# First output blocks of the last batch, worked inside the last attention unit and between the last attention products

## The reference

```python
scale, shift = split(emb @ W_emb + b_emb)             # emb is cond
xn = rms_norm(x, g_norm) * (1 + scale) + shift
q, k, v = heads(xn @ W_qkv);  q, k = rms_norm(q, g_q), rms_norm(k, g_k)
o = softmax(q @ k.T / 8) @ v                           # per head
x = x + o + o @ W_out
x = x + (causal depthwise conv1d(x, w=cond, 4 taps) + b_conv)
```

## Time and profile before

| | before |
|---|---|
| time, median of 3 executions | 2622.6 us (2620.4 to 2622.89) |
| the profiled execution | 2618.81 us |
| its span | 2616.9 us |
| mean granted TensorE clock | 0.958 of full |
| PE busy | 2372.9 us, 91% |
| DVE busy | 2106.6 us, 80% |
| ACT busy | 1815.4 us, 69% |
| POOL busy | 660.5 us, 25% |

### The profile page before, as it was taken

How to read it: one execution, slowest core, us unless ns; L and a number is a source line. 1 busy time by engine, 2 the same in 40 slices (tenths; PEclk the granted TensorE clock), 3 DMA queues, 4 the chain that set the end, 5 groups by cost and what they waited for, 6 DMA issues and landing times.

```text
span 2616.9 us, 54024 instructions
## 1 busy us (share of the span) xinstructions
PE 2372.9 (91%) x20690; PEld 1527.4 (58%) x20690; DVE 2106.6 (80%) x3360; ACT 1815.4 (69%) x2823; POOL 660.5 (25%) x460
## 2 busy tenths in 40 slices
PE   1458998888889999999999999999999999999698
PEld 0034555555556666666666666666666666666487
DVE  6757777777778888888888888888888888888845
ACT  2237777777777877777777778777777777877611
POOL 0052322223222233222233232332222222222000
PEclk8879989989989999999999999999999999999789
DMA  6877988989999999999999999999988989887841
GB/s 236 344 192 152 172 166 174 180 173 179 218 197 183 185 203 184 193 190 219 205 206 193 200 187 189 196 186 229 193 176 171 179 162 182 165 164 155 158 150 61
DMA packets 1234881, 487.07 MB, mean 186 GB/s; under 512 B 1139521, under 2 KB 1196993, under 8 KB 1232065
## 3 DMA queue, kind: packets, MB, share of 16 engines
q1 hardware_dynamic: 1234624, 483.63, 87.8%
HBM read 141.13 MB, written 57.18 MB: 76 GB/s over the span
## 4 chain that ended last, share of the span: by engine, by line
PE 69%; DVE 11%; issue 6%; ACT 4%; SPq 3%; DMA 1%; POOL 0%; ACTq 0%; DVEq 0%
PE proj L774 36%; PE scores L723 11%; PE values L742 10%; PE proj L798 8%; DVE neg L1178 5%; DVE p_pair L1187 4%; SPq L576 3%; ACT p_pair L896 2%; PE proj L801 1%; PE misc L811 1%; DVE bias L1181 1%; ACT prob L888 1%; PE misc L786 1%; PE values L757 1%; PE values L749 1%
## 5 line engine op out<-in xcount | busy, mean ns | idle before, releaser
L774 PE MATMUL proj<-w_sb,xn_sb 128*128 128x384 f16 x6144 | 1029.4, 327 | 33.9 <-DMA xn_sb<-p_pair 29.1
L888 ACT ACTIVATE prob<-scores,bias,l_scale 128x1024 f32<-128x1024 f32 x512 | 615.5, 1203 | 353.7 <-DVE bias L1181 336.0
L774 PEld LDWEIGHTS proj<-w_sb,xn_sb 128*128 128x128 f16 x6144 | 588.9, 98 | 434.0 <-DMA xn_sb<-p_pair 25.6
L1178 DVE TENSOR_REDUCE neg<-scores 128x1 f32<-128x1024 f32 x512 | 623.8, 1218 | 156.1 <-PE scores L723 152.3
L1187 DVE TENSOR_TENSOR p_pair<-prob,p_pair 128x1024 f16<-128x1024 f32 x512 | 614.8, 1242 | 137.6 <-ACT p_pair L896 137.6
L896 ACT ACTIVATE p_pair<-prob 128x1024 f16<-128x1024 f32 x512 | 511.0, 1049 | 0.4 <-DMA pT<-p_pair 0.4
L723 PE MATMUL scores<-stack 64*128 64x512 f16 x3072 | 391.4, 389 | 58.8 <-ACT prob L888 57.1
L742 PE MATMUL values<-pT,v_pair 128*64 128x256 f16 x6144 | 396.9, 280 | 11.0 <-DMA pT<-p_pair 6.3
L742 PEld LDWEIGHTS values<-pT,v_pair 128*64 128x64 f16 x6144 | 324.2, 112 | 93.5 <-issue 78.6
L1102 POOL TENSOR_TENSOR rs<-ms,power 128x16 f32<-128x16 f32 x64 | 185.6, 2900 | 395.6 <-DVE ms L1201 395.6
L1131 POOL TENSOR_TENSOR oT_pair<-oT,oT_pair 128x256 f16<-128x256 f32 x128 | 148.7, 1162 | 541.4 <-ACT oT_pair L965 541.4
(11 more groups left out here) (127 smaller groups left out, 2089.3 us busy)
## 6 DMA issues: line engine op xcount, KB each, us to landing
w_sb<-w_dram SPq DMA_DIRECT2D x128, 384.0 KB, 4.1
o_dram<-oT_pair SPq DMA_DIRECT2D x128, 128.0 KB, 2.5
out<-acc SPq DMA_DIRECT2D x64, 256.0 KB, 2.7
wq_raw<-in_L_cond_W_qkv SPq DMA_DIRECT2D x8, 1536.0 KB, 10.6
w_dram<-wq_pair SPq DMA_DIRECT2D x8, 1536.0 KB, 7.4
x_in<-in_x SPq DMA_DIRECT2D x24, 512.0 KB, 4.4
oT_in<-o_dram SPq DMA_DIRECT2D x12, 1024.0 KB, 6.0
xr<-in_x SPq DMA_DIRECT2D x24, 512.0 KB, 4.1
```

What stands on the lines that cost most here:

```text
L774: last = nc.tensor.matmul(proj[:, t % 2, 0:6 * DH], xn_sb[:, t, i * K + c, :], w_sb[:, c, j, :], start=(c == 0 and i == j == 0), stop=(c = ...
L888: nc.scalar.activation(prob[:, h, :], scores[:, h, :], ACT.Exp, bias=bias[:, s:s + 1], scale=const["l_scale"][:, 0:1], accum_out=total[:, ...
L1178: nc.vector.tensor_reduce(neg[:, s:s + 1], scores[:, h, :], axis=AX.X, op=ALU.max, negate=True).then_inc(max_done, 1)
```

## The change

It only touches unit 31 (`last = u + 1 == U`) and the tail. Block 23's products move from stages 5 to 7 to stages 1 (first half) and 3 (second half), its `xr` is loaded at the start of stage 0, and its convolutions run in stages 4 to 7. `last_xr` 0 to 2 are loaded in stage 0, `last_oT[0]` in stage 6. Block 24 is worked on PE in stages 6 and 7 (`tail_product`), block 25 between the attention products of the tail; the tail's loop then begins with block 26. The reads, convolutions, transposes and stores follow. The diff, cut to its core:

```diff
@@ SP, unit
+                    if last and p == 0:
+                        load_xr(T, par)
                     (the transposes of the stage)
+                    if last and p == 0:
+                        for i in range(3):
+                            load_last_xr(i)
                     if p == 6 and fins:
                         store_out(T - 1, 1 - par, 1)
+                    if last and p == 6:
+                        load_last_oT(0)
+                    if last and p == 7:
+                        store_out(T, par, 0)
@@ SP, tail
             for h in range(2):
                 transpose_p(U - 1, NS - 2 + h)
+            load_last_oT(1)
+            load_last_xr(3)
+            store_out(U - K - 1, 1, 1)
             store_o(U - 1, 2)
             load_last_oT(2)
+            store_out(U - K, 0, 0)
+            load_last_xr(4)
+            store_out(U - K, 0, 1)
             store_o(U - 1, 3)
             load_last_oT(3)
@@ PE
+            def tail_product(i, hh):
+                T = U - K + i
+                loaded = ((last_oT_ld[i // 2], 16), (last_xr_ld[i % 3], 16 * (i // 3 + 1)), (eye_done, U - K + 2))
+                for m in range(2):
+                    out_product(T, i % 2, hh, m, last_oT[i // 2], last_xr[i % 3],
+                                loaded + ((y_ev, 2 * T + hh - 1),))
@@ PE, unit
-                    if outs and p >= 5:
+                    if outs and p >= 5 and not last:
+                    if last and p in (1, 3):
+                        loaded = ((oT_ld, 8 * (T - par) + 16), (xr_ld, 16 * (T + 1)), (eye_done, T - par + 2))
+                        hh = p // 2
+                        free = (h_ev, 3 * U) if hh == 0 else (y_ev, 2 * T)
+                        for i in range(2):
+                            out_product(T, par, hh, i, oT_in, xr, loaded + (free,))
+                    if last and p == 6:
+                        out_transposes(T, 0, (f_ev, 2 * T))
+                    if last and p >= 6:
+                        tail_product(0, p - 6)
@@ PE, tail
             attend(U - 1, 2, 1, 1)
+            out_transposes(U - K - 1, 1, (f_ev, 2 * (U - K) - 1))
+            tail_product(1, 0)
             inverses(U - 1, 3)
+            tail_product(1, 1)
+            out_transposes(U - K, 0, (f_ev, 2 * (U - K)))
             attend(U - 1, 3, 1, 0)
             attend(U - 1, 3, 1, 1)
-            for i in range(K):
+            out_transposes(U - K, 1, (f_ev, 2 * (U - K) + 1))
+            for i in range(2, K):
@@ ACT, unit
+                    if last and p == 2:
+                        read_y(T, T - par + 2, 0)
+                    if last and p == 4:
+                        read_y(T, T - par + 2, 1)
+                    if last and p == 7:
+                        read_out(T, 0)
+                        read_y(U - K, U - K + 2, 0)
+                    (after stage 5:)
+                    if last and p == 5:
+                        scaled_eye(U - K)
@@ DVE, unit
+                    if last and p >= 4:
+                        convolve(T, par, p // 2 - 2, p % 2)
+                    if last and p == 5:
+                        set_scale(U - K)
-                    if p == 7 and outs:
+                    if p == 7 and outs and not last:
@@ DVE, tail
-            convolve(U - K - 1, 1, 0, 1)
-            for i in range(2):
-                convolve(U - K - 1, 1, 1, i)
-            scale_values(U - 1, 3)
             for T in range(U - K, U):
                 (the four convolve calls of T)
+                if T == U - K + 1:
+                    scale_values(U - 1, 3)
```

More of the change, by code:

```diff
@@ L606, in store_out, with load_last_oT, load_last_xr @@
                              fin(hh).rearrange("p (a n) -> p a n", a=2)).then_inc(f_st[hh], 16)
+            def load_last_oT(g):
+                sp.wait_ge(o_st, 16 * (NG * (U - 1) + g + 1))
+                sp.wait_ge(qkv_mm, K * U)
+                sp.dma_start(last_oT[g].rearrange("p c s n -> p c (s n)"),
+                             o_dram[((B - 1) * NG + g) * K:((B - 1) * NG + g + 1) * K].rearrange("c p n -> p c n")
+                             ).then_inc(last_oT_ld[g], 16)
+            def load_last_xr(i):
+                T = U - K + i
+                sp.wait_ge(qkv_mm, K * U)
+                if i >= 3:
+                    sp.wait_ge(op_mm, 2 * (T - 2))
+                sp.dma_start(last_xr[i % 3], x_block(T, i % 2)).then_inc(last_xr_ld[i % 3], 16)
             def unit(u, par, qkv, xs, outs, fins):
@@ L613, in unit @@
                 begun = not (static(u) and u == 0)
+                last = u + 1 == U
                 for p in range(K):
+                    if last and p == 0:
+                        load_xr(T, par)
                     for h in range(2):
@@ L624, in unit @@
                             store_o(u - 1, 2)
-                        if outs:
+                        if outs and not last:
                             load_xr(T, par)
@@ L675, in _ @@
             in_units(unit, sp, load_rows)
[L677 to L687, removed]
             for h in range(2):
                 transpose_p(U - 1, NS - 2 + h)
[L691 to L694, removed]
+            load_last_oT(1)
+            load_last_xr(3)
+            store_out(U - K - 1, 1, 1)
             store_o(U - 1, 2)
             load_last_oT(2)
-            for hh in range(2):
-                store_out(U - K - 1, 1, hh)
+            store_out(U - K, 0, 0)
+            load_last_xr(4)
+            store_out(U - K, 0, 1)
             store_o(U - 1, 3)
             load_last_oT(3)
-            for i in range(K):
+            for i in range(1, K):
                 T = U - K + i
-                if i + 3 < K:
-                    load_last_xr(i + 3)
+                if 5 <= i + 4 < K:
+                    load_last_xr(i + 4)
                 for hh in range(2):
@@ L865, in _ @@
             attend(U - 1, 2, 1, 1)
+            out_transposes(U - K - 1, 1, (f_ev, 2 * (U - K) - 1))
+            tail_product(1, 0)
             inverses(U - 1, 3)
+            tail_product(1, 1)
+            out_transposes(U - K, 0, (f_ev, 2 * (U - K)))
             attend(U - 1, 3, 1, 0)
             attend(U - 1, 3, 1, 1)
-            for i in range(K):
+            out_transposes(U - K, 1, (f_ev, 2 * (U - K) + 1))
+            for i in range(2, K):
                 T = U - K + i
-                loaded = ((last_oT_ld[i // 2], 16), (last_xr_ld[i % 3], 16 * (i // 3 + 1)), (eye_done, U - K + 2))
                 for hh in range(2):
-                    for m in range(2):
-                        out_product(T, i % 2, hh, m, last_oT[i // 2], last_xr[i % 3],
-                                    loaded + ((y_ev, 2 * T + hh - 1),))
+                    tail_product(i, hh)
                     out_transposes(T - 1, hh, (f_ev, 2 * T - 2 + hh))
@@ L1081, in _ @@
             in_units(unit, act)
-            read_y(U - K - 1, U - K, 1)
             read_inverses(U - 1, 2)
+            read_y(U - K, U - K + 2, 1)
             o_high(U - 1, 2)
+            read_out(U - K - 1, 1)
+            read_y(U - K + 1, U - K + 2, 0)
             inverse_rows(U - 1, 3)
-            scaled_eye(U - K)
+            read_y(U - K + 1, U - K + 2, 1)
+            read_out(U - K, 0)
             read_inverses(U - 1, 3)
+            read_out(U - K, 1)
             o_high(U - 1, 3)
-            for i in range(K):
+            for i in range(2, K):
                 T = U - K + i
@@ L1342, in _ @@
             scale_values(U - 1, 2)
-            set_scale(U - K)
-            convolve(U - K - 1, 1, 0, 1)
-            for i in range(2):
-                convolve(U - K - 1, 1, 1, i)
-            scale_values(U - 1, 3)
             for T in range(U - K, U):
```

## The result

The change made the kernel slower: 2632.47 us (median of 7, 2628.2 to 2635.74) against 2622.89 for the kernel before in as many executions (2619.58 to 2625.1). The ratio is 1.0036, with a 95% interval of 1.0024 to 1.0047. The forecast was 2611.8, so it was 20.7 us off and on the wrong side, outside its range.

What follows compares the result with a forecast made beforehand. PE waits for exponentials in unit 31 and bounds the tail. Landing of last_oT[0] at 2478.8, 115.0 us of PE work and 12.3 behind it give a span of 2606.1, -10.8 us; 2622.6 - 10.8 = 2611.8 us, range 2606.5 to 2618.5.

Steps and rivals of the forecast that it cites:

- Stages 1 and 3: Unit 31 on PE: block 23's halves fill holes, shifting the next scores by -0.2 us and +0.9 us.
- The rival of the low clock: Unit 31: block 23's halves run at half clock throughout, 16.1 us more than forecast, 2627.9 us; chance 0.08.
- DVE: Unit 31: three more convolutions, in stages 4, 5 and 6; +0.5 us in stage 4, hidden in stage 5.
- The wait in stage 6 for block 22's store: Unit 31 on DVE: the convolution waits about 3 us for that store, covered because stage 7's scores come later.
- The landing: Stage 6 of unit 31: last_oT[0], issued at 2472.8, takes 6.0 us and lands at 2478.8.
- PE has an unbroken list: From last_oT[0]'s landing to the last product PE works without a gap, 115.0 us, ending at 2593.8.
- What is late next: nothing, if DVE and the stores keep up: Tail: tightest is block 24's second-half transposition at 2514.9; block 23's store lands in 2.5 to 5.1 us, convolutions end 2508 to 2511.
- Late load: Stage 6: last_oT[0] lands 9.1 to 11.5 us after issue, 3.1 to 5.5 later; 2614.9 to 2617.3 us; chance 0.12.
- hole for hole: Unit 31: PE's new wait in stage 6, unhidden convolutions and a late load leave 4.0 us gain, 2618.6; no difference, chance 0.13.
- waits of the output transposes for convolutions in the tail: Tail on PE: listed among the signs in the new profile that would show the forecast wrong; no size given.

Runs made afterwards that it cites:

- experiment 1: Changed kernel with the load of last_xr[i + 4] behind block i's two output stores instead of ahead of them: 2621.73 us, ratio 0.9995 to the kernel before.
- experiment 2: Changed kernel with scale_values(31, 3) on DVE behind block 24's convolutions instead of block 25's: 2624.04 us, ratio 1.0011 to the kernel before.
- experiment 3: Changed kernel with the last_xr load behind the stores and scale_values(31, 3) behind block 24's convolutions: 2613.55 us, ratio 0.9963 to the kernel before.
- experiment 4: Kernel before with only block 23's part of the change, blocks 24 to 31 all in the tail: 2625.36 us, ratio 1.0009.
- experiment 5: Changed kernel with the two edits, and stage 7's scores, inverses and group 2's attention products ahead of block 24 on PE: 2608.29 us, ratio 0.9954.
- experiment 6: Changed kernel with the two edits, and the store of block 23's second half ahead of the last_oT[1] and last_xr[3] loads: 2611.29 us, ratio 0.9966.
- experiment 7: Kernel before with one number changed: last_xr loads from the fourth on wait for one more block of products: 2641.43 us, ratio 1.0084.
- the two edits: In the changed kernel: last_xr[i + 4] load behind block i's stores; scale_values(31, 3) behind block 24's convolutions. Together 2613.55 us.

## Why the prediction was wrong, by its own steps

**Stages 1 and 3** were sized rightly. Behind the first scores of unit 31, those of stage 2 started after 18.5 us (19.4 forecast, 19.5 before) and those of stage 4 after 35.0 (36.3 forecast, 33.7 before); in the profiles of experiments 1 to 5 it was 18.5 to 19.8 and 35.1 to 36.4. The rival of the low clock fell: block 23's halves took 6.2 and 6.4 us, and 7.1 to 7.5 in the profiles of experiments 1, 3, 4 and 5, against the over 8 for the rival's sign.

**DVE.** Stage 4 took 8.53 us instead of the 8.2 of my sum, stage 5 7.43, as said. The wait in stage 6 for block 22's store is there (4.07 us) and was covered, as said; in experiment 4 (3.20 us) it was not.

**The landing** was forecast at 63.8 and came at 64.2 us. The load itself took 7.0 us instead of 6.0, not the 9 to 11 of the rival, and its issue was 0.6 earlier than my sum had it, so the nearness of 64.2 to 63.8 is two errors that cancel in part.

**From the landing on: the step that failed.** "PE has an unbroken list" and "What is late next: nothing, if DVE and the stores keep up" were written after following one store, that of block 23, and its landing was mis-sized: 7.4 us behind the 1.5 MB of loads, not 2.5 to 5.1. That cost PE a wait of 0.93, which is gone in experiment 6. I did not follow SP's list through the tail's loop. There the change had moved `load_last_xr` by one block against the stores (`i + 4` for `i + 3` in the same place), and its wait with it: before, the load ahead of block i's stores waited for block i's own products, which were done whenever a store was ready; now it waits for block i + 1's. A first-half store is then late by about a half block of products (5.8 us in experiment 7 at full clock, 8.2 and 7.7 in the changed kernel, where the clock had fallen) and lands 2 us later, right behind the load. The ring of store, convolution, transposes and read had less slack than this in its 13.14 us, as the stalls show. The forecast also let `scale_values(31, 3)` pass without asking who stands behind it: `o_high` on ACT, and behind that ACT's `read_out`. From unit 31 the two edits give 9.0 and 7.4 us alone and 17.1 together, of the 20.1 between the changed kernel and the forecast; the other 3.0 lie half ahead of the landing (65.3 for 63.8), half behind it (116.6 for 115.0). From the landing on, the gains are 10.0, 7.2 and 18.1. Experiment 7 makes the first part alone out of the kernel before.

**The rivals.** The sign came from none of them. "Late load" and "hole for hole" were about the landing, and the landing was right. What was wanted was a rival in SP's queue in the tail, and the profile of before held the hint: SP waited there for ACT's output reads 15 times and for products never. The prediction's own list of signs did name what came: "waits of the output transposes for convolutions in the tail". It gave them no price and no chance.

What stays open: how much of the first stall is the 7 us landing of block 25's stores behind the loads. The stall shrank by 1.2 us with the first edit alone, by 4.0 with the second, and went with both; no run changed that landing by itself. Nor did a run separate, in the later stalls, the late issue of a store from its longer landing behind the load.

## What to carry to other kernels

When a loop's DMA loads are renumbered or moved against its stores on one issuing queue, compare for each store which semaphore values stand ahead of it in the queue, before and after: a load's wait that is one step later delays every store behind it, and puts the load's bytes right ahead of them. Follow each engine's list to the end of the program, and above all the issuing queue, before calling another engine's list unbroken. Filling a hole with work that has still to be waited for puts that wait in front of whatever is queued behind; put what is ready first (experiment 5, by its profile).

## What was not expected of the hardware

A wait of 2.4 to 2.8 us on PE was in most cases followed by a low clock. Between the landing and the last product there are ten such waits: two in the changed kernel, three in experiment 2 and five in experiment 7. PE had been busy without a gap for over 12 us ahead of each. In the wait itself the granted clock was still 1.00 (2563.40 to 2565.90 of the changed kernel); it fell while PE worked again. Behind eight of the ten the next 24 products took 3.83 to 4.45 us instead of 2.78; behind two, of 2.46 and 2.54 us, they took 2.78. The length of the wait does not tell which: 2.40 was followed by the low clock both times. So a stall of 2.6 us cost up to 4.5, counted from product to product (2562.71 to 2570.71, 8.00 us for the 3.50 of the undisturbed stretch), and 2.7 to 2.8 where the clock held. After the 6.77 us stall the same 24 took 4.96, after the 8.6 us hole 4.87. A store of 256 KB landed in 2.1 us alone, in 3.5 with only transposes ahead of it, in 4.0 to 4.2 right behind a 512 KB load, and in 7.4 behind 1.5 MB of loads.
